# Unread matrix products ahead of four stages of a two-layer attention and experts kernel, and one projection moved forward

## The chip, the cores and the metric

The kernel runs on one core of one Trainium2 chip, as one program. The metric is the device time of one execution in microseconds (us). Three executions of the kernel before took 1533.29, 1536.22 and 1537.31 us; the median is 1536.22 us. The engines are named as in the profile: PE (TensorE), PEld (its weight loads), DVE (VectorE), ACT (ScalarE), POOL (GpSimd), SP (SyncE, which here only issues DMAs).

## The reference

4096 tokens (32 blocks of 128) of width 256 go through two layers, each an attention and a mixture of experts, every one added to its input:

```python
x = x + L0_xattn(layernorm(x), ctx, ctx, ...)   # 16 heads, masked by token id
x = x + L0_ffn(layernorm(x), ...)               # router, top 2 of 8 experts, width 1024
x = x + L1_xattn(layernorm(x), ctx, ...)        # two attentions and a gate
x = x + L1_ffn(layernorm(x), ...)               # top 2 of 8, at most 640 tokens for each expert
```

## The kernel before, in words

The program has four stages, one after the other on every engine. Each engine runs a list of instructions written out in full; the order within an engine is the order of the calls in the code, and between engines only semaphores order the work.

- Stage A (`first_attention`, from 0 to about 400 us) runs the first attention over 32 blocks, writes the normalised rows to DRAM, and scatters token numbers to the slots of the experts. `a_pe` starts with two small transposes (line 684), and then takes the blocks in a software pipeline.
- Stage B (`first_experts`, about 400 to 826 us) runs 71 blocks of expert rows. POOL gathers slot numbers (`load_ids`, line 1175, counted in `i_ld`) and then rows (`gather`, line 1183). ACT and DVE split the rows into a high and a low f16 part. SP turns them by a DMA transpose (`xT`). PE makes the hidden layer in `up(j)` (12 products of 512 columns, line 1342, two halves, each counted in `up_done`). ACT applies silu to each half (line 1300, `silu_done`), casts the high part (line 1305, `hi_done`); DVE makes the low part (line 1273, `lo_done`); SP transposes the hidden rows (`hT`); PE makes `down(j)` (24 products, line 1355). The loop in `b_pe` calls `up(j + 1)`, `down(j - 1)` and `fold(pe, j)` for j from -1 on. The addresses of the weights hang on the expert's number, which PE loads into a register and adds up in register instructions between the products.
- Stage C (`second_attention`, about 826 to 1158 us) runs the second attention over 32 blocks. `from_ctx(b)` projects context rows into PSUM bank 0 (line 1822, counted in `ts_done`) and bank 2 (line 1828, `vs_done`). ACT takes the first out (`ctx_out`, `ts_out`), DVE the second (`vs_out`). `transpose_x(b)` (line 1849) and `from_rows(b)` do the same for the normalised rows of the stage, which wait for the gathers of the expert rows of stage B (`yg_ld`, line 1639) and for the normalisation on DVE, POOL and ACT (lines 1981 to 1989, 1648 to 1652, 1713). `scores(b)` (lines 1869 and 1872) needs both. ACT's exponential is line 1744, and `transpose_p` is line 1880. In the kernel before, `from_ctx(1)` stands behind `scores(0)`.
- Stage D (`second_experts`, about 1158 to 1530 us) runs 8 experts with 640 slots each. POOL first clears `rowsum` (line 2217, `d_clear`), waits for the slot numbers and gathers 5 blocks of 128 rows for expert 0 (line 2225). PE transposes each block (`transpose_x`, line 2269), ACT and DVE split it into f16 parts (lines 2331 and 2374), and both must be done before the next transpose may write the same bank. The hidden width is taken in 8 units; `up(e, p, fc, q)` (line 2285) makes a unit's products in three pieces q of 256, 256 and 128 columns, 12 products each; `down` is line 2298. ACT's silu is line 2339.

## Time and profile before

| | us |
|---|---|
| median of three runs (1533.29 to 1537.31) | 1536.22 |
| the profiled execution | 1534.38 |
| its span, first to last instruction | 1532.6 |
| outside its span | 1.8 |
| PE busy (89%) | 1356.7 |
| PEld busy (72%) | 1100.2 |
| DVE busy (55%) | 847.2 |
| ACT busy (53%) | 816.1 |
| POOL busy (44%) | 671.5 |

Start times below are us from the start of the span. Busy time of PE is modelled: products overlap, and one product's duration is longer than the distance to the next one. "[7.44 <-ACT qeo L558]" in a row means that the engine had been idle for 7.44 us, and that ACT's instruction on `qeo` at line 558 released it.

### The profile page before, as it was taken

What the parts mean: (1) busy time and instruction counts of PE and PEld (TensorE: products, weight loads), DVE (VectorE), ACT (ScalarE), POOL (GpSimd) and SP (SyncE); (2) the same over time, 40 slices, a digit from 0 to 9 for tenths busy, and PEclk for the clock granted to TensorE, in tenths of its full rate; (3) what the DMA queues carried; (4) which work ended last, traced back from release to release, by engine and by line L of the source; (5) the groups of instructions that cost most, each with busy time, mean ns of one, the idle gap of its engine ahead of it and who ended that gap; (6) DMA issues with size and microseconds to landing.
All of it is one profiled execution on the core that took longest, in us unless ns stands there. A gap on an engine that the chain in (4) does not pass through costs nothing.

```text
span 1532.6 us, 37450 instructions
## 1 busy us (share of the span) xinstructions
PE 1356.7 (89%) x12922; PEld 1100.2 (72%) x12922; DVE 847.2 (55%) x2350; ACT 816.1 (53%) x1904; POOL 671.5 (44%) x935
## 2 busy tenths in 40 slices
PE   5999999997169999999996899999982999999996
PEld 4787777775136666667664888888871888888985
DVE  4787788776423222332231677777762566666663
ACT  3787778775035555554552555555541545454442
POOL 3234545454453333333302456666655344444322
PEclk8999999999579999999998999999995999999998
DMA  3333435442059999988885223332222333343331
GB/s 113 111 113 98 121 94 103 108 90 54 21 112 178 201 193 182 183 169 149 161 160 121 69 84 84 83 84 83 81 64 57 109 124 113 123 130 104 127 104 50
DMA packets 280856, 172.76 MB, mean 113 GB/s; under 512 B 212990, under 2 KB 259424, under 8 KB 280676
## 3 DMA queue, kind: packets, MB, share of 16 engines
q1 hardware_dynamic: 257940, 134.65, 38.8%
q0 software_dynamic: 18608, 32.14, 7.7%
q10 hardware_dynamic: 4128, 3.57, 0.8%
q8 instruction: 112, 1.84, 0.6%
q14 instruction: 68, 0.56, 0.2%
HBM read 93.40 MB, written 31.80 MB: 82 GB/s over the span
## 4 chain that ended last, share of the span: by engine, by line
PE 81%; issue 4%; ACT 4%; DVE 3%; DMA 3%; POOL 2%; another core or an unknown queue 1%; ACTq 0%; SPq 0%; DVEq 0%; POOLq 0%
PE psum L2285 14%; PE psum L1355 12%; PE psum L1342 11%; PE psum L2298 7%; PE psum L1822 4%; PE psum L1903 4%; PE psum L1828 3%; PE psum L747 2%; PE psum L805 2%; PE psum L734 2%; PE psum L708 2%; PE psum L822 2%; PE psum L1893 2%; PE psum L808 2%; PE psum L786 2%
## 5 line engine op out<-in xcount | busy, mean ns | idle before, releaser
L1273 DVE SCALAR_TENSOR_TENSOR b_h<-b_hid,b_h 128x1024 f16<-128x1024 f32 x71 | 87.0, 1225 | 280.6 <-ACT b_h L1305 274.7
L2285 PE MATMUL psum<-d_xT,d_w 128*128 128x256 f16 (+1 forms) x2304 | 231.5, 257 | 5.3 <-DVE d_xT L2374 2.9
L1342 PE MATMUL psum<-arena,b_xT 128*128 x852 | 200.2, 386 | 28.0 <-DMA b_xT<-b_x 27.6
L2285 PEld LDWEIGHTS psum<-d_xT,d_w 128*128 128x128 f16 x2304 | 200.1, 99 | 24.1 <-DVE d_xT L2374 2.5
L1355 PE MATMUL psum<-arena,b_hT 128*128 x1704 | 200.5, 274 | 13.9 <-DMA b_hT<-b_h 8.8
L1355 PEld LDWEIGHTS psum<-arena,b_hT 128*128 128x128 f16 x1704 | 166.0, 98 | 52.9 <-issue 20.2
L1342 PEld LDWEIGHTS psum<-arena,b_xT 128*128 128x128 f16 x852 | 84.3, 99 | 119.1 <-issue 36.6
L1300 ACT ACTIVATE b_hid<-psum 128x512 f32<-128x512 f32 x142 | 84.7, 597 | 136.3 <-PE psum L1342 85.6
L1183 POOL DMA_INDIRECT b_xg<-dram_normed,b_gi x71 | 67.1, 945 | 205.2 <-DVE b_x L1266 193.6
L2339 ACT ACTIVATE d_sg<-psum 128x256 f32<-128x256 f32 (+1 forms) x192 | 65.8, 348 | 147.7 <-PE psum L2285 136.3
L2384 DVE SCALAR_TENSOR_TENSOR d_hf<-psum,d_sg 128x256 f32<-128x256 f32 (+1 forms) x192 | 71.0, 379 | 107.8 <-ACT d_sg L2339 89.3
L2298 PE MATMUL psum<-d_w,d_h 128*128 128x256 f16 x960 | 115.3, 273 | 2.3 <-issue 1.6
L602 ACT ACTIVATE pT<-psum,amc 128x512 f32<-128x512 f32 x128 | 77.6, 689 | 48.5 <-PE psum L734 43.3
L2298 PEld LDWEIGHTS psum<-d_w,d_h 128*128 128x128 f16 x960 | 91.2, 98 | 15.3 <-issue 4.8
L1639 POOL DMA_INDIRECT c_yg<-dram_expert_rows,c_gi x64 | 65.0, 1015 | 69.9 <-DMA dram_expert_rows<-b_ys 54.9
L949 DVE TENSOR_REDUCE mx<-psum 128x4 f32<-128x512 f32 x128 | 79.4, 682 | 27.4 <-PE psum L708 25.5
L2242 POOL DMA_INDIRECT d_rowsum<-out,d_gi x40 | 44.7, 1118 | 91.6 <-PE psum L2285 67.8
L1175 POOL DMA_INDIRECT b_gi<-dram_ids,ypos x71 | 68.6, 967 | 31.4 <-issue 31.4
L2247 POOL DMA_INDIRECT out<-d_rowsum,d_gi x40 | 41.8, 1045 | 92.4 <-DVE d_rowsum L2399 85.1
L1305 ACT ACTIVATE b_h<-b_hid 128x1024 f16<-128x1024 f32 x71 | 75.0, 1057 | 4.7 <-DMA b_hT<-b_h 2.5
L1674 POOL DMA_INDIRECT dram_ids<-c_gsidw,c_gsidx x64 | 68.0, 1063 | 19.4 <-issue 19.4
L477 POOL DMA_INDIRECT dram_ids<-tokens,gsidx x64 | 67.5, 1054 | 12.6 <-issue 12.6
(316 smaller groups left out, 2930.4 us busy)
## 6 DMA issues: line engine op xcount, KB each, us to landing
d_wst<-in_L_w SPq DMA_DIRECT2D x64, 384.0 KB
stage<-in_L_w SPq DMA_DIRECT2D x32, 512.0 KB
dram_expert_rows<-b_ys SPq DMA_DIRECT2D x71, 128.0 KB
ctxT<-in_ctxT SPq DMA_DIRECT2D x64, 128.0 KB
dram_normed<-xn SPq DMA_DIRECT2D x64, 128.0 KB
x<-in_x SPq DMA_DIRECT2D x32, 128.0 KB, 5.8
dram_x<-xnew SPq DMA_DIRECT2D x32, 128.0 KB
c_x<-dram_x SPq DMA_DIRECT2D x32, 128.0 KB
```

Of the source, the lines that this page charges most:

```text
L602: act.activation(pT[:, r, :, :].rearrange("p j q -> p (j q)"), psum[:, SB + r, :], ACT.Exp, bias=amc[:, b:b + 1]).then_inc(exp_done[r], 1)
L949: i = dve.tensor_reduce(mx[:, r, :], psum[:, SB + r, :].rearrange("p (j k) -> p j k", j=HB), AX.X, ALU.max)
L1175: pool.indirect_dma_start(gi[:, j % NX, :], None, ids[0], bass.IndirectOffsetOnAxis(ap=ypos[:, j:j + 1], axis=0)).then_inc(i_ld[j % NX], 16)
L1273: dve.scalar_tensor_tensor(out=h16[:, p, 1, :], in0=hid[:, p, :], scalar=H_SCALE, in1=h16[:, p, 0, :], op0=ALU.mult, op1=ALU.subtract).the ...
L1300: act.activation(hid[:, p, half * 512:(half + 1) * 512], psum[:, 1 + 2 * p + half, :], ACT.Silu, scale=1.0 / (X_SCALE * W_SCALE)).then_inc ...
L1305: act.activation(h16[:, p, 0, :], hid[:, p, :], ACT.Copy, scale=H_SCALE).then_inc(hi_done, 1)
L1342: i = pe.matmul(psum[:, 1 + 2 * p + half, :], xT[:, j % NT, px, c, :], weights(e, c, pw, half * 512, 512), start=(n == 0), stop=(n == len( ...
L1355: i = pe.matmul(psum[:, 6 + p, 0:D], hT[:, p, ph_, c, :], weights(e, 2 + c // 4, pw, (c % 4) * D, D), start=(n == 0), stop=(n == len(terms ...
L1674: pool.indirect_dma_start(ids[1], bass.IndirectOffsetOnAxis(ap=gsidx[:, g % 3, at:at + 1], axis=0), gsidw[:, g % 3, at, :], None, bounds_c ...
L2285: i = pe.matmul(psum[:, q, m * n:(m + 1) * n], w16[:, fc % RING, pw, col:col + P], xT[:, p, px, c, at:at + n], start=(k == 0), stop=(k == ...
L2298: i = pe.matmul(psum[:, NQ + k, 0:D], h16[:, fc % 2, ph_, k * P:(k + 1) * P], w16[:, fc % RING, pw, 2 * DC * P:UW], start=(fc == 0 and t = ...
L2384: dve.scalar_tensor_tensor(out=hf[:, fc % 2, at:at + n], in0=psum[:, q, n:2 * n], scalar=H_SCALE / (X_SCALE * W_SCALE), in1=sg[:, fc % 2, ...
```

## The change

`keep_on(pe, bank, n)` issues n products of the f16 identity with itself, 128 columns each, into a bank of PSUM that is overwritten before anybody reads it. Each has its own weight load. It is called in stage A behind the two small transposes (36), in stage B ahead of `up(0)` once the first slot numbers are there (60) and between `up(1)` and `up(2)` in three parts (24, 20, 40) that each wait for a step of block 0, in stage C ahead of the first transpose, once the first gathered rows are there (36), and in stage D behind POOL's clearing of `rowsum` (56) and behind each of the five transposes of expert 0 (10 each). That is 332 products. In stage C `from_ctx(1)` comes directly behind `from_ctx(0)`, with ACT's `ctx_out(1)` and DVE's `vs_out(0)` and `vs_out(1)` moved to the front of their lists as well.

```diff
--- before.py
+++ after.py
@@ -172,6 +172,11 @@
         def due(v):
 
             return not isinstance(v, int) or v > 0
+
+        def keep_on(pe, bank, n):
+
+            for _ in range(n):
+                pe.matmul(psum[:, bank, 0:P], ident16[:, :], ident16[:, :], start=True, stop=True)
 
         class Steps:
 
@@ -683,6 +688,7 @@
                 for k in range(2):
                     i = pe.transpose(psum[:, 2, k * NB:(k + 1) * NB], rows_f[:, k, :], ident[0:NB, 0:NB])
                 i.then_inc(rowt_done, 1)
+                keep_on(pe, 7, 36)
 
                 def penalty(b, r, n):
 
@@ -1356,8 +1362,15 @@
                                           start=(n == 0), stop=(n == len(terms) - 1))
                         i.then_inc(down_done, 1)
 
+                pe.wait_ge(i_ld[0], 16)
+                keep_on(pe, 5, 60)
                 for j in range(-1, N_B + 1):
                     up(j + 1)
+                    if j == 0:
+
+                        for steps, n in ((silu_done, 24), (hi_done, 20), (lo_done, 40)):
+                            pe.wait_ge(steps, 2 if steps is silu_done else 1)
+                            keep_on(pe, 5, n)
                     down(j - 1)
                     fold(pe, j)
 
@@ -1792,16 +1805,18 @@
                         act.wait_ge(w_ready, g)
                     act.activation(ge[:, 0:n], gd[:, 0:n], ACT.Exp).then_inc(ge_ready, 1)
 
+                ctx_out(0)
+                ctx_out(1)
                 normalise_x(0)
                 xnT_out(0)
-                ctx_out(0)
                 normalise_x(1)
                 rows_out(0)
                 xnT_out(1)
                 for b in range(NB + 2):
                     expo(b)
                     normalise_x3(b - 2)
-                    ctx_out(b + 1)
+                    if b > 0:
+                        ctx_out(b + 1)
                     gate(b - 1)
                     x2T_out(b - 2)
                     pT_out(b)
@@ -1831,7 +1846,9 @@
                 def from_ctx(b):
                     if inside(b):
                         pe.wait_ge(ctx_ld[b % 2], nth(b))
-                        if due(b):
+                        if b == 1:
+                            pe.wait_ge(ts_out, 1)
+                        if due(b - 1):
                             pe.wait_ge(tc_out, b)
                         project(ms, ctxT[:, b % 2, :, :], 0).then_inc(ts_done, 1)
                         if due(b):
@@ -1852,7 +1869,7 @@
                 def from_rows(b):
                     if inside(b):
                         pe.wait_ge(xnT_ready, b + 1)
-                        pe.wait_ge(ts_out, b + 1)
+                        pe.wait_ge(ts_out, max(b + 1, 2))
                         project(mc, xT[:, b % 2, :, :], D).then_inc(tc_done, 1)
                         if due(b):
                             pe.wait_ge(vc_ready, b)
@@ -1950,6 +1967,9 @@
                 pe.wait_ge(fold_out, 2)
                 pe.wait_ge(col_out, 1)
                 from_ctx(0)
+                from_ctx(1)
+                pe.wait_ge(yg_ld[0], 32)
+                keep_on(pe, 5, 36)
                 transpose_x(0)
                 from_rows(0)
                 transpose_x(1)
@@ -1957,7 +1977,8 @@
                     if last_of(b - 3) is not None:
                         count(last_of(b - 3))
                     scores(b)
-                    from_ctx(b + 1)
+                    if b > 0:
+                        from_ctx(b + 1)
                     gate(b - 1)
                     transpose_x3(b - 2)
                     transpose_p(b)
@@ -2122,8 +2143,9 @@
                         dve.wait_ge(scat[g % 3], scattered(g - 3))
                     dve.tensor_copy(gsidx[:, g % 3, 0:2 * n], gslot[:, 0:2 * n]).then_inc(slot_ready, 1)
 
+                vs_out(0)
+                vs_out(1)
                 add_experts(0)
-                vs_out(0)
                 add_experts(1)
                 vc_out(0)
                 for b in range(NB + 3):
@@ -2138,7 +2160,8 @@
                     top(b - 2)
                     if last_of(b - 2) is not None:
                         hots(last_of(b - 2))
-                    vs_out(b + 1)
+                    if b > 0:
+                        vs_out(b + 1)
                     vc_out(b + 1)
                     residual(b - 1)
             return c_sync, c_pool, c_act, c_pe, c_dve, load_weights, scaled, first_rows, fold_pe, fold_act, fold_dve
@@ -2306,6 +2329,7 @@
                             if e == 0 and fc == 0:
                                 for k in range(2 * q, min(2 * q + 2, CBLK)):
                                     transpose_x(0, 0, k)
+                                    keep_on(pe, NQ + CBLK - 1, 10)
                             if q == NQ - 1 and 1 <= fc <= CBLK and is_expert(e + 1):
                                 pe.wait_ge(h_ready, NQ * (e * FC + fc))
                                 transpose_x(e + 1, 1 - p, fc - 1)
@@ -2314,6 +2338,8 @@
                             up(e, p, fc, q)
                         down(e * FC + fc - 1, (fc - 1) % FC, e)
 
+                pe.wait_ge(d_clear, 1)
+                keep_on(pe, NQ + CBLK - 1, 56)
                 for e in range(E):
                     body(e, e % 2)
                 down(E * FC - 1, FC - 1, E - 1)
```

## Rows read from the trace of the kernel before

**Rows 1.** The page's slices of the span: the granted clock of PE, in tenths.
```profile
PEclk8999999999579999999998999999995999999998
```

**Rows 2.** Windows: stretch, its length, busy us of each engine, clock, DMA share, GB/s.
```profile
422.30:427.20 4.90, 4.79 (x12) 1.86 (x13) 0.42 (x1) 2.30 (x3) 3.68 (x5) 0.50 0.45 104
427.20:437.50 10.30, 6.91 (x39) 3.40 (x37) 1.56 (x2) 2.56 (x4) 8.17 (x8) 1.00 0.53 115
...
833.40:843.60 10.20, 4.59 (x16) 3.74 (x17) 3.57 (x10) 2.72 (x7) 5.32 (x9) 0.50 0.18 53
...
1178.90:1185.00 6.10, 3.98 (x17) 2.57 (x18) 0.85 (x2) 0.77 (x2) 2.12 (x3) 0.50 0.24 65
1185.00:1188.40 3.40, 1.44 (x12) 0.93 (x11) 0.85 (x2) 0.77 (x2) 1.93 (x2) 1.00 0.13 39
...
1340.00:1360.00 20.00, 20.00 (x209) 18.24 (x207) 12.01 (x24) 9.96 (x22) 4.95 (x5) 1.00 0.36 114
```

**Rows 3.** Timeline of stage A: start, us, engine line op out<-in, count, idle before.
```profile
17.94 0.75 POOL L463 TENSOR_SCALAR other<-tokr,tokc 128x128 f32<-128x128 f32 x1 [9.48 <-DMA tokr<-dram_tokens]
...
22.98 0.66 PE L776 MATMUL psum<-ident,xn 128*128 128x128 f32 x2 [7.44 <-ACT qeo L558]
```

**Rows 4.** Timeline of the start of stage C.
```profile
833.89 0.48 DVE L1981 SCALAR_TENSOR_TENSOR c_ytmp<-c_yg,routew,c_x 128x256 f32<-128x256 f32 x1 [14.48 <-DMA c_yg<-dram_expert_rows,c_gi]
...
837.93 0.69 PE L1849 MATMUL psum<-ident,xn 128*128 128x128 f32 x2 [9.53 <-ACT xn L1713]
...
839.70 2.04 PE L1822 MATMUL psum<-c_xT,c_Wq_c 128*128 128x128 f32 x8 [1.08 <-ACT c_tsT L1728]
...
841.03 0.60 ACT L1713 ACTIVATE xn<-c_x,rstd 128x256 f32<-128x256 f32 x1 [1.47 <-POOL rstd L1652]
...
841.54 1.92 PE L1828 MATMUL psum<-c_Wv_c,c_xT 128*128 128x257 f32 x4
...
844.57 1.06 PE L1822 MATMUL psum<-ctxT,c_Wq_s 128*128 128x128 f32 x8
...
847.20 0.45 PE L1880 MATMUL psum<-ident,c_pr 128*128 128x128 f32 x2 [0.70 <-DVE c_pr L2010]
```

**Rows 5.** Timeline of the start of stage D.
```profile
1171.52 1.17 POOL L2217 MEMSET d_rowsum<- 128x1280 f32 x1 [1.78 <-DMA dram_ids<-c_gsidw,c_gsidx]
...
1178.97 0.69 PE L2269 MATMUL psum<-ident,d_xg 128*128 128x128 f32 x2 [20.65 <-DMA d_xg<-dram_normed,d_gi]
...
1182.37 2.72 PE L2285 MATMUL psum<-d_xT,d_w 128*128 128x256 f16 x12 [1.02 <-DVE d_xT L2374]
...
1192.93 3.89 PE L2285 MATMUL psum<-d_xT,d_w 128*128 128x256 f16 x24 [0.33 <-DVE d_hf L2384]
...
1196.88 0.83 PE L2285 MATMUL psum<-d_xT,d_w 128*128 128x128 f16 x12
...
1199.18 2.78 PE L2285 MATMUL psum<-d_xT,d_w 128*128 128x256 f16 x24
```

**Rows 6.** Timeline of the start of stage B.
```profile
411.80 1.00 POOL L1175 DMA_INDIRECT b_gi<-dram_ids,ypos  x1 [10.06 <-issue]
...
422.40 10.31 PE L1342 MATMUL psum<-arena,b_xT 128*128 x36 [27.58 <-DMA b_xT<-b_x]
...
423.71 1.28 ACT L1300 ACT_TABLE_LOAD   x1
...
434.99 0.60 ACT L1300 ACTIVATE b_hid<-psum 128x512 f32<-128x512 f32 x1 [5.42 <-remote]
...
436.11 2.30 PE L1355 MATMUL psum<-arena,b_hT 128*128 x15 [3.39 <-DMA b_hT<-b_h]
...
440.38 0.94 POOL L1175 DMA_INDIRECT b_gi<-dram_ids,ypos  x1 [0.30 <-issue]
...
444.10 0.60 ACT L1300 ACTIVATE b_hid<-psum 128x512 f32<-128x512 f32 x1 [8.52 <-remote]
```

**Rows 7.** Line 1342 alone, 415 to 460 us: durations in ns, min/median/max.
```profile
L1342 PEldq FUSED_REGOPS  x41: 3/46/692, 422.3 to 460.0; - x41
```

## The prediction

> **What bounds the kernel now.** I read the slices of the clock first, then windows over the stretches where it is low, then the timeline there. The slices show PE at 8 to 10 tenths except where one stage ends and the next begins, near 400, 830 and 1170 us [rows 1]. Inside the last stage PE is the bound: 20.00 us busy in a window of 20 [rows 2]. So a microsecond that PE gains at the start of stage D is not given back later. At the starts PE waits for gathered rows, for 27.58 us in stage B, 9.53 us in C and 20.65 us in D [rows 4 to 6], and begins its first work at a clock of 0.50, which is 1.2 GHz: 422.3 to 427.2, 833.4 to 843.6 and 1178.9 to 1185 us [rows 2]. The change can win only the time by which this first work is slower than at 2.4 GHz, and only where that work, not another engine, ends last.
>
> **Price of an unread product.** At the full clock, 12 products of 128 columns took 0.83 us and 24 of 256 took 2.78 us [rows 5]. The tail is the same, so 35 steps of 128 columns cost 1.95 us: 0.056 us each. At half clock I take twice that, 0.11 us; the 12 of 256 columns in 2.72 us [rows 5] agree (22 steps of 0.11 us and a tail of 0.3).
>
> **Stage A, 36 products.** 4.0 us behind the two small transposes, with up to 0.7 us of delay for the first block's transpose. What stands behind is block -2's work of the pipeline, and then PE idles for 7.44 us until 22.98 us, since POOL's mask waited 9.48 us for a DMA until 17.94 [rows 3]. Both the gain and the delay end in that idle time. Value 0. Bounds: without this cover a delay of 0.7 us; a gain is excluded, as the DMA chain hangs on DVE.
>
> **Stage B, 60 products and then 84.** The first slot numbers land between 412.8 and 415.6 us (POOL's first issue ends at 412.8 [rows 6]). Sixty products at half clock are 6.6 us, so they end at 422.2 at the latest, just ahead of `up(0)` at 422.40 [rows 6]. The 24 products of `up(0)` and `up(1)` then run at up to twice the speed. But ACT loads its table until 424.99 [rows 6] and takes out the first half only after that, so the second half's silu moves from 427.6 to 425.8 at best: 1.8 us. That is lost or kept at the next wait. What is late next is not the clock: ACT stood for 5.42 us until 434.99 and for 8.52 us until 444.10 for an event that the profile can't name [rows 6], though the 36 products that it waited for are recorded as over at 432.71. In the same stretch PE's register instructions between the products took up to 692 ns against a median of 46 [rows 7]. POOL was issuing indirect DMAs all that time, 23 from 411.80 to 440.38, one each 1.25 us [rows 6]; the hold-up begins after the clock rose at 427.2 and ends some 3 us after POOL's last issue. If it ends by POOL's schedule, an earlier start gains nothing: value 0. The 84 products between `up(1)` and `up(2)` wait for block 0's low part, ready about 430.5. At full clock the last 40 are 2.2 us and `up(2)` some 2.6, so PE is at `down(0)` at 435.4, and its data came at 436.11 [rows 6]: hidden by 0.7 us. At half clock they are 4.4 and 5.1 us: 3.9 us late, in front of ACT's second wait that lasted to 444.10. Bounds of stage B: 12 us gained (if the hold-up goes) to 8 us lost (below).
>
> **Stage C, 36 products and the moved projection.** At 0.50, the two transposes took 0.69 us, the projection 2.04 and the value product 1.92 [rows 4]. At full clock the pair of transposes takes 0.45 and the eight projection products 1.06 [rows 4]; the value product goes to about 1.0. But the chain goes by the later of PE and the normalisation of block 1. ACT's `xn` of block 1 starts at 841.03, released by POOL [rows 4], and neither POOL's list nor its gathers move, so it ends at 841.63 as before. The second transpose started at 843.25, behind the value product (841.54 + 1.92, less overlap) [rows 4]; now it can start at 841.65. Scores of block 0 and all that follows move by 1.6 us. The 36 products (4.0 us from about 833.9) end at 837.9, when the transpose comes (837.93 [rows 4]); if they end late, the delay is under 0.3 us. The moved `from_ctx(1)` goes to PE's idle time before the rows. From where it stood (844.57, 1.06 us and some 1.0 more [rows 4]) it takes nothing off the path, as PE still waited 0.70 us for `c_pr` [rows 4] that DVE makes. It passes no DMA. On ACT, `ctx_out(0)` and `ctx_out(1)` come in idle time; on DVE the two `vs_out` wait for products that end by 831, before the rows at 833.89 [rows 4]. Value 1.6 us gained; bounds 0.5 lost (late products) to 2.5 gained (all of 0.24 + 0.98 + 0.9 and a little more, if `xn` were earlier too).
>
> **Stage D, 56 and 50 products.** POOL's clearing ends at 1172.69, and 56 products at half clock take 6.2 us, to 1178.9; the first transpose is at 1178.97 [rows 5]. The ten behind each transpose lie under the trip through ACT and DVE that the next transpose waits for anyway (1.0 us at full clock with the transpose itself, against 1.7 us between the first two). Gain along the path, piece by piece at 2.4 GHz: two transposes ahead of the first `up`, 0.25 each; `up` of piece 0 from 2.72 to half of 2.78 and a tail, about 1.5: 1.2; piece 1, which ran at mixed clock, 0.6; last transpose, 0.2; then 24 products of the next unit from 3.89 to 2.78 [rows 5], of which the transpose among them leaves 1.2. Sum 3.7 us. Pieces on ACT (table load, silu) keep their length. Bounds: 0 (clock stays low) to 4.5.
>
> A page of the Trainium skill speaks against both starts. The row first: between 1185 and 1188.4 us the clock was 1.00, PE worked 1.44 us in pieces with waits between them, and it was 0.50 again afterwards [rows 2]; so a burst with waits lost the full clock once it had it. "TensorE: Matmul & The Clock Gate", section "HAM oscillation — how this bites in real kernels", says the same of kernels whose products come in short bursts between waits. By that rule the starts stay bursts, the sum is the 2.5 us of rival 3 and the time 1533.7; by the ten products that fill the waits of stage D it is 5.3 us. The granted clock of the one stretch bears the rule out, but there the waits were empty.
>
> **Sum.** 0 + 0 + 1.6 + 3.7 = 5.3 us. Against the profiled execution's own time of 1534.38 that gives 1529.1; it is 1.8 us under the median of the runs, 1536.2, so for the median 1530.9. I say 1531.
>
> **Rivals.**
> 1. *The hold-up in stage B gets longer: slower.* Its place is PE's instruction stream while POOL issues its 23 DMAs. It began 1.3 us after the clock rose. With a warm PE from about 420 us and 60 dense products in front, it would begin some 8 us earlier (420 against 428.5), before the silu of block 0, and still end with POOL at about 444. Then block 0's hidden rows are transposed only when block 1's were before, and the pipeline is one block behind at least. A block is 24 products of 256 columns and 12 of 512, 48 steps of 256 columns at 0.109 us: 5.2 us. A second block lost would be 10.4; I take 8: 1531 + 8 = 1539. It decides from 5.3 us, where it eats the gains of C and D. For it: 692 ns instructions only with the dense warm stream [rows 7]. Against it: the unread products have no register instructions between them.
> 2. *The hold-up goes away.* Spacing PE's work differently could avoid it. Then `lo_done` of block 1 comes at 433 instead of 447, less 2 us for the DMA queue: 11 to 12 us, and 1531 - 11 = 1520. For it: nothing but that its cause is unknown.
> 3. *The clock doesn't stay up.* In stage D it falls after the first transposes, as at 1188.4; in stage C PE is now idle from about 843 to 845.6, where `from_ctx(1)` had been, so the clock may fall there instead, and the next projection pair costs 2 us more, half of it under waits. Stage D then keeps 1.9 of 3.7 and stage C 0.6 of 1.6: 2.5 us, 1533.7.
> 4. *The unread products do not raise the clock at all*: stage B to D as before, small delays: 1536. Speaks against it: plain f16 products raised the clock at 427.2 [rows 2].
>
> **How the numbers follow.** This kernel's measurement can tell 0.3%, 4.6 us: faster is under 1531.6. Chances: forecast 0.42, rival 1 0.20, rival 2 0.13, rival 3 0.20, rival 4 0.05. The forecast's own spread is about 3 us either way, since stage B's wait is not exact; some 0.30 of its 0.42 lies under 1531.6. With rival 2 and a little of rival 3 that is 0.45 faster. Same, 1531.6 to 1540.8: the rest of the forecast, rivals 3 and 4, and the lighter part of rival 1 (a loss of up to 8 us in stage B ends inside), 0.41. Slower 0.14, where two blocks or more are lost. The range: 1522 leaves out the lower part of rival 2, 1539.5 the upper part of rival 1; the likeliest case alone has 1528 to 1534.
>
> **What would show it.** Right: the granted clock at 1.0 from about 837 and 1178 us on; 843.25 for the second transpose of stage C becoming 841.6; the piece of 12 products in stage D at 1.5 us and its successor of 24 at 2.8. ACT's two unnamed waits in stage B end near 435 and 444. Wrong: those waits shorter or later by over 3 us, a clock of 0.5 within 1179 to 1190 or 844 to 851, or a first transpose in stage D later than 1179.5.

## The result, and the profile after

| | before | after |
|---|---|---|
| median of 20 runs each | 1532.99 us (1526.23 to 1538.14) | 1540.82 us (1536.64 to 1546.74) |
| profiled execution | 1534.38 us | 1544.04 us |
| its span | 1532.6 us | 1542.3 us |

The ratio of after to before is 1.0056, with a 95% interval of 1.0043 to 1.007: the change made the kernel slower, by 7.8 us between the medians and by 8.6 us by the ratio. The forecast was 1531, with a range of 1522 to 1539.5. From one group of runs to the next the kernel before took from 1509 to 1544 us, so kernels are compared within their group only, by the ratio; where an experiment's difference is given in us, it is the ratio times the group's median of the kernel before.

The page of the kernel after, busy time of PE and the slices of its clock:

```profile
PE 1382.9 (90%) x13244; PEld 1128.4 (73%) x13244; DVE 848.7 (55%) x2350; ACT 816.7 (53%) x1904; POOL 670.6 (43%) x935
...
PEclk8999999998579999999999899999996999999998
```

PE is busy 26 us longer than before, and the clock's slices hardly differ from [rows 1]. It executes 322 products more, 13244 against 12922: the change adds 36 + 60 + 84 + 36 + 56 + 50 = 322, not 332. Where the time went is read from the start times of the same step in both traces. The profiled execution after was 9.7 us longer: 5.4 us of it were there at POOL's first slot gather of stage B (411.80 and 417.20), 6.3 came up to the `down` of block 10, 5.9 in the rest of stage B. Stage C gave back 1.8 and stage D 6.1.

Of the 6.1 us of stage D only 2.1 lie where the change could reach, from the first transpose to the 97th product of `up`. The other 4.1 come behind it and are not the change's: in all 17 traces this rest of stage D takes either 312.6 to 313.9 us or 317.1 to 317.9, and in each group of the experiments all kernels lie on one level, with and without the change; only this first pair of traces lies on both. The 5.9 us in the rest of stage B can't be put down to the change either: it takes 334.3 us before and 340.3 after, and from 334.1 to 341.7 in the other kernels that leave POOL alone there (331.8 to 333.5 with POOL held, below).

The start of stage B after, a timeline (columns as in [rows 3]; line 1348 is `up`, 1361 `down`, 179 the unread products):

```profile
417.20 1.00 POOL L1181 DMA_INDIRECT b_gi<-dram_ids,ypos  x1 [8.80 <-issue]
...
420.06 5.07 PE L179 MATMUL psum<-ident 128*128 128x128 f16 x60 [18.59 <-DMA b_gi<-dram_ids,ypos]
...
428.02 3.84 PE L1348 MATMUL psum<-arena,b_xT 128*128 x17 [2.89 <-issue]
...
434.33 0.38 PE L1348 MATMUL psum<-arena,b_xT 128*128 x1 [1.72 <-issue]
...
442.31 0.94 POOL L1181 DMA_INDIRECT b_gi<-dram_ids,ypos  x1 [0.31 <-issue]
...
445.53 0.59 PE L1348 MATMUL psum<-arena,b_xT 128*128 x1 [1.51 <-issue]
447.05 1.08 ACT L1306 ACTIVATE b_hid<-psum 128x512 f32<-128x512 f32 x2 [16.55 <-PE psum L1348]
...
448.19 7.65 PE L179 MATMUL psum<-ident 128*128 128x128 f16 x84 [2.08 <-ACT b_hid L1306]
...
458.27 2.78 PE L1361 MATMUL psum<-arena,b_hT 128*128 x24
```

Beside [rows 6]: the 60 products end in time, and `up(0)` begins at full clock. After 17 products of `up` PE gets one product each 2.1 us, while POOL issues a DMA each 1.25 us; "issue" says that PE waited for nothing that the profile shows. It ends some 5 us after POOL's last issue. ACT's silu of block 0 waits 16.55 us, where ACT had waited twice, 5.42 and 8.52 us. Then the 84 products take 7.65 us, and `down(0)` is at 458.27 instead of 436.11.

Windows of the kernel after (columns as in [rows 2]), the ones of stage B first:

```profile
428.00:432.00 4.00, 3.84 (x17) 1.68 (x18) 0.42 (x1) 1.70 (x2) 3.07 (x4) 1.00 0.47 113
432.00:446.00 14.00, 3.35 (x7) 0.61 (x6) 0.00 (x0) 0.00 (x0) 8.52 (x9) 0.68 0.18 47
```
```profile
845.00:848.00 3.00, 2.93 (x17) 2.04 (x15) 0.44 (x2) 1.25 (x4) 0.95 (x1) 1.00 0.33 96
848.00:851.40 3.40, 0.00 (x0) 0.00 (x0) 0.41 (x1) 0.00 (x0) 2.48 (x4) 0.80 0.39 119
851.40:855.50 4.10, 4.01 (x37) 3.82 (x38) 3.16 (x8) 0.60 (x1) 2.35 (x5) 0.50 0.19 57
...
1191.40:1200.00 8.60, 4.51 (x63) 3.95 (x62) 0.85 (x2) 0.77 (x2) 4.79 (x6) 1.00 0.49 165
```

From 432 to 446 PE starts 7 products and 6 weight loads, and ACT and DVE nothing at all. In stage C the moved projection ends at full clock before 848; PE is empty until the rows land, and the 36 products and the first transpose run at 0.50. The starts of stages C and D, timelines after, for [rows 4] and [rows 5]:

```profile
851.47 0.48 DVE L2002 SCALAR_TENSOR_TENSOR c_ytmp<-c_yg,routew,c_x 128x256 f32<-128x256 f32 x1 [3.06 <-DMA c_yg<-dram_expert_rows,c_gi]
...
851.49 4.02 PE L179 MATMUL psum<-ident 128*128 128x128 f16 x36 [3.55 <-DMA c_yg<-dram_expert_rows,c_gi]
...
855.44 0.69 PE L1866 MATMUL psum<-ident,xn 128*128 128x128 f32 x2
...
856.60 2.08 PE L1837 MATMUL psum<-c_xT,c_Wq_c 128*128 128x128 f32 x8 [0.47 <-ACT c_xT L1733]
...
860.18 0.43 PE L1866 MATMUL psum<-ident,xn 128*128 128x128 f32 x2
```
```profile
1188.63 4.58 PE L179 MATMUL psum<-ident 128*128 128x128 f16 x56 [14.43 <-POOL d_rowsum L2240]
...
1194.75 0.44 PE L2292 MATMUL psum<-ident,d_xg 128*128 128x128 f32 x2 [1.54 <-DMA d_xg<-dram_normed,d_gi]
...
1199.27 1.47 PE L2308 MATMUL psum<-d_xT,d_w 128*128 128x256 f16 x12 [1.94 <-DVE d_xT L2400]
...
1207.75 2.78 PE L2308 MATMUL psum<-d_xT,d_w 128*128 128x256 f16 x24 [0.94 <-DVE d_hf L2410]
```

### The profile page after: what moved, and what is told of

It is laid out like the page before. It is cut to its first block, busy times and chain, and to the rows that moved or that the text cites. A ratio compares the mean times of both kernels' runs of the same rounds, so it can differ in the third digit from the quotient of the medians.

```text
span 1542.3 us, 38095 instructions
## 1 busy us (share of the span) xinstructions
PE 1382.9 (90%) x13244; PEld 1128.4 (73%) x13244; DVE 848.7 (55%) x2350; ACT 816.7 (53%) x1904; POOL 670.6 (43%) x935
## 4 chain that ended last, share of the span: by engine, by line
PE 80%; DVE 5%; issue 5%; DMA 4%; ACT 4%; POOL 2%; another core or an unknown queue 0%; ACTq 0%; SPq 0%; DVEq 0%; POOLq 0%
PE psum L2308 14%; PE psum L1348 11%; PE psum L1361 11%; PE psum L2321 7%; PE psum L1837 3%; PE psum L1843 3%; PE psum L1920 3%; PE psum L811 2%; PE psum L753 2%; PE psum L740 2%; PE psum L828 2%; DMA b_hT<-b_h 2%; PE psum L714 2%; PE psum L814 2%; PE psum L1910 2%
## 5 line engine op out<-in xcount | busy, mean ns | idle before, releaser
L2308 PE MATMUL psum<-d_xT,d_w 128*128 128x256 f16 (+1 forms) x2304 | 227.1, 255 | 3.6 <-DVE d_xT L2400 2.7
L2308 PEld LDWEIGHTS psum<-d_xT,d_w 128*128 128x128 f16 x2304 | 198.3, 98 | 22.6 <-issue 3.2
L1361 PEld LDWEIGHTS psum<-arena,b_hT 128*128 128x128 f16 x1704 | 166.4, 98 | 43.9 <-issue 10.8
L1348 PEld LDWEIGHTS psum<-arena,b_xT 128*128 128x128 f16 x852 | 83.6, 98 | 105.1 <-issue 22.6
L2321 PEld LDWEIGHTS psum<-d_w,d_h 128*128 128x128 f16 x960 | 91.0, 98 | 11.7 <-issue 1.0
L955 DVE TENSOR_REDUCE mx<-psum 128x4 f32<-128x512 f32 x128 | 79.5, 683 | 22.8 <-PE psum L714 22.7
```

The costliest lines, as they stand in the source:

```text
L955: i = dve.tensor_reduce(mx[:, r, :], psum[:, SB + r, :].rearrange("p (j k) -> p j k", j=HB), AX.X, ALU.max)
L1348: i = pe.matmul(psum[:, 1 + 2 * p + half, :], xT[:, j % NT, px, c, :], weights(e, c, pw, half * 512, 512), start=(n == 0), stop=(n == len( ...
L1361: i = pe.matmul(psum[:, 6 + p, 0:D], hT[:, p, ph_, c, :], weights(e, 2 + c // 4, pw, (c % 4) * D, D), start=(n == 0), stop=(n == len(terms ...
L2308: i = pe.matmul(psum[:, q, m * n:(m + 1) * n], w16[:, fc % RING, pw, col:col + P], xT[:, p, px, c, at:at + n], start=(k == 0), stop=(k == ...
L2321: i = pe.matmul(psum[:, NQ + k, 0:D], h16[:, fc % 2, ph_, k * P:(k + 1) * P], w16[:, fc % RING, pw, 2 * DC * P:UW], start=(fc == 0 and t = ...
```

## The experiments

While it issues them back to back, PE and ACT get their instructions slowly, about one each 0.70 us on PE (a weight load, a register instruction and a product make the 2.1 us above). PE lives on what it has in hand; every unread product takes two instructions of that. **Rivals.** The clock: a warm, dense PE brings the hold-up on. The products' own time: the 84 stand in the way.

The table has all kernels; a group is named by the median of the kernel before in it. "Start of B" is from POOL's first slot gather to the `down` of block 10; "start of C" from `add_experts(0)` to the first softmax (its maximum on DVE); "D" from its first transpose to its last product, "its start" from there to the 97th product of `up`. The ratios come from 6 to 20 executions of each kernel, these columns from the one that was profiled, and that one lies up to 8.6 us from its kernel's median.

| kernel | group | ratio to before (95%) | A, block 31 at | start of B | start of C | D | its start |
|---|---|---|---|---|---|---|---|
| before | 1533 | | 386.6 | 87.8 | 10.9 | 340.8 | 23.0 |
| after | 1533 | 1.0056 (1.0043 to 1.007) | 393.2 | 94.0 | 10.1 | 334.6 | 21.0 |
| without B's products | 1536 | 1.0007 (0.9987 to 1.0028) | 389.6 | 87.6 | 10.2 | 333.7 | 20.8 |
| 60 of B alone | 1536 | 1.0043 (1.002 to 1.0065) | 397.2 | 94.3 | 10.6 | 336.0 | 23.2 |
| 15 wide in B | 1536 | 1.0006 (0.9988 to 1.0025) | 390.7 | 89.2 | 11.7 | 338.4 | 24.6 |
| POOL held | 1536 | 0.9914 (0.989 to 0.9937) | 392.1 | 77.3 | 11.8 | 337.0 | 23.0 |
| 36 of A alone | 1541 | 1.0036 (1.0021 to 1.0051) | 396.1 | 88.6 | 11.7 | 340.9 | 23.2 |
| 84 of B alone | 1541 | 1.0031 (1.0017 to 1.0045) | 389.9 | 93.9 | 11.8 | 340.4 | 23.0 |
| C and D alone | 1541 | 0.9988 (0.9969 to 1.0007) | 391.3 | 88.5 | 9.0 | 338.7 | 21.1 |
| after, POOL held | 1541 | 0.9947 (0.9926 to 0.9969) | 392.0 | 79.8 | 9.1 | 339.9 | 22.6 |
| held, C warm, D | 1509 | 0.9934 (0.9915 to 0.9953) | 378.7 | 76.9 | 9.0 | 333.0 | 20.4 |
| 9 wide in A | 1509 | 1.0002 (0.9983 to 1.0021) | 382.8 | 79.3 | 10.8 | 335.6 | 23.0 |
| POOL spaced | 1509 | 1.0005 (0.9986 to 1.0024) | 380.9 | 77.4 | 10.3 | 333.9 | 21.3 |
| spaced, again | 1544 | 1.0005 (0.9989 to 1.0021) | 394.4 | 90.1 | 11.8 | 342.2 | 24.3 |
| held, C warm, D, again | 1544 | 0.9887 (0.9865 to 0.9908) | 394.2 | 77.2 | 9.7 | 339.3 | 22.3 |
| 9 wide in A, again | 1544 | 0.9995 (0.9981 to 1.0008) | 386.4 | 88.9 | 10.5 | 340.8 | 23.2 |
| held, again | 1544 | 0.9902 (0.9884 to 0.992) | 391.2 | 78.7 | 10.6 | 342.5 | 24.7 |

**Without B's products.** The two groups of calls taken out of `b_pe`; the rest as after.

```diff
-                pe.wait_ge(i_ld[0], 16)
-                keep_on(pe, 5, 60)
...
-                    if j == 0:
...
-                            keep_on(pe, 5, n)
```

> The changed kernel without both groups of unread products of stage B (60 and 84); those of stages A, C and D and the moved projection stay. Theory 1, the loss is made in stage B (from its first slot-number gather to its tenth down it lost 6.3 us, and some 3 more by its end): the time is that of the kernel before less what C (0.8 us) and D (2.5 us at its start) gained, so 2 to 4 us faster than before. Rival, the 36 products of stage A shift its pipeline (stage A was 6.6 us longer in the profile after): then this kernel is still 2 to 4 us slower than before, and its block 31 of stage A ends near 393 us and not near 387.

The 0.56% are gone: the loss hangs on stage B's products. But the gain of 2 to 4 us wasn't there either (1.1 us slower, interval 2.0 faster to 4.3 slower), and neither was the rival's loss of 2 to 4. So something else in the rest may cost.

**60 of B alone**, and **15 wide**: the kernel before with only

```diff
+                pe.wait_ge(i_ld[0], 16)
+                keep_on(pe, 5, 60)
```
or, in the same place, 15 products with a moving side of 512 columns (the identity read four times by a stride of 0):
```diff
+            wide = rows(ident16[:, :], 4)
...
+                pe.matmul(psum[:, bank, :], ident16[:, :], wide, start=True, stop=True)
```

> The kernel before with only the 60 unread products of stage B. Theory 1, instruction supply: while POOL issues its indirect DMAs back to back PE gets one instruction each 0.70 us as soon as the ones it has in hand are used up; before this happened after some 140 instructions (from 438 us), in the kernel after at 432 us after some 176, of which 120 belonged to the 60 products. So these 60 alone are enough: PE's instructions 0.70 us apart from about 427 us (time of the kernel before) to about 443, inside up(1), the first lo part of block 1 a block (5.2 us) later than in the kernel before, and 4 to 7 us slower. Rival, the loss came of the 84 products (7.65 us at half clock between up(1) and up(2)): then this kernel takes the time of the one before within 1 us, or is 1 us faster.

> As the kernel with the 60 products alone, but the same columns in 15 products of 512 (30 instructions instead of 120), at the same place and for the same time on PE. Theory 1, the number of instructions counts: PE runs short no earlier than without unread products, so no block is lost, the time is that of the kernel before within 1.5 us, and the clock is full from about 421 us all the same. Rival, the warm clock (PE's own rate and its register instructions at full clock) brings the hold-up on: then it is as slow as the kernel with 60, 4 to 7 us over the kernel before.

Timeline of the 60, then of the 15 wide with its window:

```profile
440.27 0.38 PE L1347 MATMUL psum<-arena,b_xT 128*128 x1 [1.72 <-issue]
...
451.60 0.60 ACT L1305 ACTIVATE b_hid<-psum 128x512 f32<-128x512 f32 x1 [16.60 <-PE psum L1347]
```
```profile
418.24 5.21 PE L185 MATMUL psum<-ident 128*128 128x512 f16 x15 [19.20 <-DMA b_gi<-dram_ids,ypos]
...
446.28 0.37 PE L1366 MATMUL psum<-arena,b_hT 128*128 x1 [1.73 <-issue]
```
```profile
426.00:434.20 8.20, 8.04 (x36) 3.44 (x36) 1.99 (x3) 4.26 (x6) 6.37 (x7) 1.00 0.39 91
```

The 60 kept PE busy for 5.38 us, the 15 for 5.21, in the same place. The 60 cost 0.43%, the 15 nothing that can be measured. With the 15 all 36 products of `up(0)` to `up(2)` went through in 8.04 us at clock 1.00, and the shortage began only in `down(0)`, as in the kernel before; with the 60 it began 17 products into `up`, though the clock there was the lower one:

```profile
432.50:438.00 5.50, 5.24 (x17) 2.10 (x18) 0.43 (x1) 1.70 (x2) 4.05 (x5) 0.74 0.44 108
```

So the clock is not the cause: with the same columns, the same time on PE and the full clock earlier, what differs is the number of instructions. ACT's hold-up came with the 15 too (8.66 us until 440.01), as in the kernel before; what the 60 added is PE's shortage inside `up`. The total is the weaker half of this: the two were compared in one group only, and their intervals overlap a little (from 1.002 on, and up to 1.0025).

**POOL held.** The kernel before, and POOL's issues tied to PE's pace:

```diff
                 for j in range(N_B):
+                    if 5 <= j < N_B:
+                        pool.wait_ge(up_done, 2 * (j - 4))
                     load_ids(j + 2)
                     gather(j)
```

> The kernel before with POOL held back in stage B: from block 5 on its next two indirect DMAs wait until up(j-4) is done; no unread products. POOL then issues some 12 back to back and not 23, and the rest at PE's pace of 5.2 us a block. Theory 1, PE is short of instructions because of POOL's back-to-back issues: the stretch with PE's instructions 0.70 us apart (438 to 444 us) goes, ACT's two unnamed waits (5.42 and 8.52 us) shrink, and the kernel is 5 to 12 us faster than before. Rival, the hold-up has another cause (the DMAs of weights, the address arithmetic of PE): the stretch stays where it was, the time within 1.5 us, or slower if the gathers now come late for PE.

The first burst has 12 issues instead of 23; the kernel is 0.86% faster, 13 us, and 0.98%, 15 us, in another group, each a little more than forecast. ACT's two waits ahead of block 1's silu, line 1302 here, are now 0.26 and 0.90 us:

```profile
435.80 0.60 ACT L1302 ACTIVATE b_hid<-psum 128x512 f32<-128x512 f32 x1 [0.26 <-PE psum L1344]
437.29 0.60 ACT L1302 ACTIVATE b_hid<-psum 128x512 f32<-128x512 f32 x1 [0.90 <-PE psum L1344]
```

So the largest loss at this place is in the kernel before too, and holding POOL back ends it.

**36 of A alone, 84 of B alone, C and D alone**: the kernel before with one part of the change each; for C and D all of the change's diff but these lines:

```diff
                 i.then_inc(rowt_done, 1)
+                keep_on(pe, 7, 36)
...
                     up(j + 1)
+                    if j == 0:
+
+                        for steps, n in ((silu_done, 24), (hi_done, 20), (lo_done, 40)):
+                            pe.wait_ge(steps, 2 if steps is silu_done else 1)
+                            keep_on(pe, 5, n)
```

> The kernel before with only the 36 unread products of stage A. Theory, they do nothing: block 0 of stage A ends at 49.3 us as in both profiles, the spread of stage A's end (386.6 to 397.2 us over six kernels, two with these products at 393.2 and 389.6, four without at 386.6, 397.2, 390.7 and 392.1) is chance, and the time is that of the kernel before within 1.5 us. Rival, they cost what the kernel without stage B's products lacks against its expected 2 to 4 us gain: then 2 to 5 us slower.

> The kernel before with only the 84 unread products of stage B (168 instructions of PE between up(1) and up(2)). Theory 1, every instruction counts while PE gets one each 0.70 us: the products stand in PE's way from about 433 us, less than half are through by the time that POOL's burst ends (about 441), and down(0) comes 8 to 12 us later than its 436.1; block 1's lo part keeps its time or comes earlier, so 3 to 6 us slower in all. Rival, they lie in idle time (they wait for ACT and DVE, and down(0) for the transposed rows): the time of the kernel before within 1.5 us.

> The kernel before with the changes of stages C and D alone: the moved projection and 36 products in C, 56 and 50 products in D. From the profiles so far C's start takes 0.8 to 0.9 us less (add_experts to the first softmax 10.88 us before, 10.07 after) and stage D 334.6 and 333.7 us from its first transpose to its last product with the change, 336.0 to 340.8 without it. Theory: C gains 0.8 and D 2.5 to 4: 3 to 5 us faster. Rival: D's shorter time is chance, as it gains only 1 us at its first piece, and what is left is within 1.5 us of the kernel before.

The 36 products of stage A cost 5.5 us, a little more than the rival's 2 to 5, where I had forecast nothing. The 84 cost 4.8 us, as theory 1 said, and put `down(0)` 40.0 us behind POOL's first gather instead of 24.3: later by 15.7 us, not by the 8 to 12 forecast. C and D alone are 1.8 us faster (4.8 faster to 1.1 slower): less than the theory's 3 to 5, and not to be told from the rival's nothing. In the 36's trace, stage A shows the mark of stage B's hold-up:

```profile
345.86 1.08 POOL L482 DMA_INDIRECT dram_ids<-tokens,gsidx  x1 [0.18 <-issue]
...
347.87 1.00 POOL L482 DMA_INDIRECT dram_ids<-tokens,gsidx  x1 [0.17 <-issue]
349.17 0.97 POOL L482 DMA_INDIRECT dram_ids<-tokens,gsidx  x1 [0.30 <-issue]
351.33 0.60 ACT L616 ACTIVATE oT<-psum 128x512 f32<-128x512 f32 x1 [6.77 <-remote]
...
351.98 1.11 PE L762 MATMUL psum<-ident,oT 128*128 128x128 f32 x4 [6.22 <-ACT oT L616]
```

ACT stands 6.77 us for something that the profile can't name, while POOL issues three scatters close together. In other traces such a wait of 3 to 7 us falls on other blocks between 345 and 395 us, and block 31 ends anywhere from 386 to 397 (397.2 in the kernel with the 60 of B alone, which has no product in stage A). So the 36's loss is shown by the totals, and not where in stage A it falls.

**9 wide in A**: the same columns as the 36, in 9 products of 512.

```diff
                 i.then_inc(rowt_done, 1)
+                keep_on_wide(pe, 7, 9)
```

> The kernel before with stage A's unread columns in 9 products of 512 instead of 36 of 128: the same time on PE, 18 instructions instead of 72. The 36 products alone made the kernel 0.36% slower (5.5 us, 0.21 to 0.51%), though block 0 of stage A kept its time (49.32 us) and the loss came in blocks 24 to 31. Theory 1, the number of instructions of PE ahead of the pipeline shifts where its later shortages fall: with 18 the time is that of the kernel before within 2 us. Rival, the products' time or the clock shifts the pipeline: then 3 to 7 us slower, as with the 36.

> Stage A's unread columns in 9 products of 512, the rest as the kernel before. The 36 products of 128 cost 0.36% where the kernel before took 1541 us; the 9 cost 0.02% where it took 1509. If the number of instructions counts: within 2 us of the kernel before, also where it takes 1533 to 1541 us. If their time on PE does: 3 to 7 us slower.

Twice nothing (1.0002 and 0.9995), where the 36 cost 0.36%. The first of the two came in the group without the hold-up and says little; the second came with it, though not beside the 36. The same columns in 18 instructions instead of 72 cost nothing that can be measured. Which later step pays for the 72 isn't shown; one profile each can't separate it from the spread of stage A.

**After, POOL held.** The whole change with the two lines of the held POOL.

> The changed kernel with all its unread products, and POOL held back in stage B from block 5 on as in the kernel that took 12 us less. Theory 1, the unread products of stage B cost time only because PE is short of instructions while POOL issues back to back: then they cost nothing here (the 60 end before the rows, the 84 lie in PE's wait for the transposed hidden rows, but for 1 to 2 us), and the time is that of the held kernel less C's and D's gains, 11 to 16 us faster than before. Rival, they cost time of their own (7.65 us at half clock between up(1) and up(2)): then it is 3 to 8 us slower than the held kernel, 4 to 9 us faster than before.

8.2 us faster than before: the rival's forecast (4 to 9), not theory 1's (11 to 16). B's start takes 79.8 us, against 77.3 and 78.7 held without products and 94.0 in the kernel after: of the 6.3 us that the products cost there, 1.2 to 2.6 are left when POOL is held. The rest of the 5 to 7 us by which this kernel lags behind the held one is not traced; the 36 of stage A are in it. The hold-up is short here, but it is there: PE runs short after 18 products of `up`, at the same place as in the kernel after, and has its instructions again 3.3 us after the last issue of POOL's first burst, at 431.19:

```profile
433.05 0.38 PE L1350 MATMUL psum<-arena,b_xT 128*128 x1 [0.88 <-issue]
434.45 1.24 PE L1350 MATMUL psum<-arena,b_xT 128*128 x5 [1.02 <-issue]
```

**POOL spaced.** Behind each issue of blocks 2 to 11 POOL fills an unused tile twice:

```diff
                     load_ids(j + 2)
+                    if 2 <= j < 12:
+                        space(2 * j - 4)
                     gather(j)
+                    if 2 <= j < 12:
+                        space(2 * j - 3)
```

> The kernel before with POOL's indirect DMAs of stage B spaced: behind each from block 2 to block 11 POOL fills an unused tile twice (some 1 us), and waits for nothing. The issues come some 2.4 us apart instead of 1.25, in the same number and order. Theory 1a, what holds PE and ACT up is the rate of POOL's issues: ACT's waits of 5.42 and 8.52 us go, and the kernel is 5 to 12 us faster than before. Theory 1b, it is their number ahead of use, whatever the rate: the stretch comes later but is as long, and the time is within 2 us of the kernel before or slower.

> POOL's indirect DMAs of blocks 2 to 11 of stage B spaced by two fills of an unused tile each, as before. The first comparison came where the kernel before took 1508.8 us, and a kernel of that group with POOL unchanged in stage B (the one with 9 wide products) had no wait of ACT over 3 us at the start of stage B: it could not tell. Where the kernel before shows its usual 1533 to 1541 us: theory 1a (the rate of the issues) 5 to 12 us faster than before; theory 1b (their number ahead of use) within 2 us or slower.

The first comparison couldn't tell, as there was no hold-up in its group (the 9 wide of that group: 79.3 us at the start of B, no wait of ACT over 3 us after the first rows). In the second the time was again that of the kernel before: theory 1b's forecast, and not the 5 to 12 us of 1a. The windows of this trace show where the time went:

```profile
444.60:473.90 29.30, 29.21 (x206) 20.16 (x207) 11.65 (x18) 16.66 (x29) 25.75 (x39) 1.00 1.01 181
473.90:482.90 9.00, 8.86 (x58) 5.48 (x56) 2.08 (x4) 2.78 (x5) 6.80 (x8) 1.00 0.93 156
483.00:492.00 9.00, 2.19 (x7) 0.67 (x7) 0.00 (x0) 0.00 (x0) 5.58 (x6) 0.74 0.18 45
```

As long as the issues came 2.2 us apart, PE was never short (29.21 us busy of 29.3), and block 4's low part was ready 37.6 us after the first gather instead of 48.4. The spacing ended at 473.97; POOL then issued each 1.25 us to 489.16, and 9 us into that PE had 7 products in 9 us, and ACT none:

```profile
492.67 0.38 ACT L1323 ACTIVATE b_ys<-psum 128x256 f32<-128x256 f32 x1 [14.34 <-remote]
```

The 11 us gained at the start were lost there. So the hold-up moves to where POOL issues back to back, and both the time and the later place are what 1b forecast. That it is the rate and not the number of blocks by which POOL leads is likely, but not shown. For it: in the kernel after PE ran short with five blocks gathered and one `up` done, a lead of four, while the held kernels have a lead of up to five through all of stage B and three of them no hold-up. Against it: while the issues were spaced the lead stayed at four or less, so this run doesn't part the two.

**Held, C warm, D.** POOL held, nothing in A and B, stage D as after, and in stage C PE kept busy across the wait for the rows:

```diff
                 from_ctx(1)
-                pe.wait_ge(yg_ld[0], 32)
-                keep_on(pe, 5, 36)
+                keep_on(pe, 5, 60)
+                pe.wait_ge(yg_ld[0], 32)
+                keep_on(pe, 5, 56)
```

> POOL held back in stage B as before; no unread products in stages A and B; stage D as in the changed kernel; in stage C the moved projection, 60 unread products right behind it (before the rows land) and 56 after. In the changed kernel the clock fell again at 850.0 us, between the moved projection (over at 847.9) and the 36 products (from 851.49), and the first transposes ran at half clock. Theory: with PE kept busy across the wait for the rows the clock is full from the rows to the first softmax, and that stretch (from add_experts, 10.88 us before, 10.07 in the kernel after, 8.95 in the one with C and D alone) takes 8.5 to 9.2 us; with D's 3 us and the held POOL's 12 the kernel is 14 to 18 us faster than before. Rival: what fills the stretch is the chain through DVE, POOL and ACT and not the clock, and it stays at 10; 12 to 15 us faster.

> POOL held back in stage B, stage C with the moved projection and 60 and 56 products, stage D as in the changed kernel. At 1508.8 us for the kernel before it was 10 us faster. If the hold-up is back (kernel before at 1533 to 1541 us): 14 to 18 us faster than before, and 3 to 6 us faster than the held kernel without C and D, which runs beside it. Rival, C and D bring nothing that can be measured: as fast as the held kernel within 1.5 us.

> The kernel before with POOL held back from block 5 of stage B on, as in the run that was 12 us faster, beside the spaced one: if the hold-up is there it is 9 to 14 us faster again, and tells whether this comparison is one in which the spaced kernel can be judged; if it is not there, it is within 3 us of the kernel before.

The timeline of the second of these at the start of stage C:

```profile
823.99 1.03 PE L1837 MATMUL psum<-c_Wv_s,ctxT 128*128 128x257 f32 x4
824.86 3.98 PE L179 MATMUL psum<-ident 128*128 128x128 f16 x65
...
829.88 2.95 PE L179 MATMUL psum<-ident 128*128 128x128 f16 x50 [0.51 <-issue]
832.68 0.39 PE L1860 MATMUL psum<-ident,xn 128*128 128x128 f32 x2
834.76 1.16 PE L1831 MATMUL psum<-c_xT,c_Wq_c 128*128 128x128 f32 x8 [1.70 <-ACT c_xT L1727]
```

The transposes take 0.39 us and the projection 1.16, against 0.69 and 2.08 in the kernel after. Yet the start of C takes 9.0 and 9.7 us, no less than with C and D alone (9.0), where the clock was 0.50 from 842.6 to 849.4. The first lies in the theory's range and the second nearer to the rival's 10; that the chain through ACT, DVE and POOL fills the rest is the likely reason and isn't shown. It is the fastest version: 0.66% under the kernel before in the group without the hold-up, and 1.13%, 17 us, in the one with it; there it is 2.3 us under the held kernel, a difference inside the intervals and under the 3 to 6 forecast.

## Why the prediction was wrong, point by point

**Stage A, 0 us.** Failed. Block 0 was not delayed (49.31 and 49.33 us), as forecast, and still the 36 products cost 5.5 us. The step looked for a cover at the place where they stand; what they spend, 72 instructions, has its price later.

**Stage B, 0 us.** This is the step that failed most: "if it ends by POOL's schedule, an earlier start gains nothing: value 0". It does end by POOL's schedule (3 to 6 us after the last issue of a burst), and an earlier start isn't free: 120 instructions of unread products make PE run short while it is still in `up`, where ACT waits for it. 0.43% (6.6 us) measured for the 60 alone, 0.31% (4.8 us) for the 84 alone. Each lies inside the step's bound of 8 us lost; the value 0 was wrong. I read the register instructions of 692 ns [rows 7] as the mark of a dense warm stream; in the kernel after these took 46 ns, and it was the weight loads and products that came late. The rows that told more were ACT's two waits for nothing named [rows 6]: two engines late at once, which nothing of PE's own work explains.

**Rival 1** is what happened, with its sign, its place and about its size: it gave 8 us for stage B alone and 1539; the start of B lost 6.3 us and the total came to 1540.8 against 1533.0. Its reason, the clock, was wrong: the wide products had the same clock and lost nothing. So was its start 8 us earlier: ACT began to stand 17.8 us after POOL's first issue before, and PE ran short 15.0 us after it in the kernel after. Against it I had set that "the unread products have no register instructions between them"; that had no bearing. Its 0.20 was too small, as the cover of the 84 products was 0.7 us by my own sum.

**Rival 2**, the hold-up goes away: not by this change, but its price of 11 to 12 us was about right, as holding POOL shows (13 and 15 us).

**Stage C, 1.6 us.** The size was about right: over the profiles of all groups but the one at 1509 us, the start of C takes 9.6 us on average with the changes (five kernels) and 11.3 without (nine), 1.7 less. In the profile after it was 0.8, since the clock was lost between 848 and 851.4, while PE stood 3.55 us for the rows, a place that the prediction hadn't named. The second transpose came 8.7 us behind the first rows instead of 9.4 in the kernel before and 7.8 as forecast. The place that rival 3 did name, the idle time where `from_ctx(1)` had been, lost the clock as well, and the eight projection products behind it took 1.91 us instead of 1.06:

```profile
863.97 0.69 PE L1897 MATMUL psum<-ident,c_pr 128*128 128x128 f32 x2 [2.47 <-DVE c_pr L2031]
864.45 1.91 PE L1837 MATMUL psum<-c_xT,c_Wq_c 128*128 128x128 f32 x8
```

So rival 3 held in stage C of this execution. The Trainium skill, page "TensorE: Matmul & The Clock Gate", section "HAM oscillation — how this bites in real kernels", warns of just such bursts with waits between. The window of stage C agrees (0.80 while PE stood 3.55 us, then 0.50).

**Stage D, 3.7 us.** The right way, but mis-sized: to the 97th product of `up` the five kernels with the changes take 21.6 us on average (20.8 to 22.7) and the nine without 23.6 (23.0 to 24.7), again without the group at 1509: 2.0 gained. The whole of D, 337.2 against 339.9, says 2.6, but the two levels of its rest are in that. The piece of 12 took 1.47 us as forecast and the later 24 took 2.78; the first transpose was found at full clock. Two terms failed. The ten products were to lie under the trip through ACT and DVE; but with them the first `up` starts 3.9 to 4.7 us behind the first transpose, and 3.4 in every kernel without them. In the kernel after, ACT took out the second pair of transposes at 1198.28, 1.5 us after it was over; what held ACT is not shown:

```profile
1196.36 0.41 PE L2292 MATMUL psum<-ident,d_xg 128*128 128x128 f32 x2 [0.61 <-issue]
...
1198.28 0.38 ACT L2357 ACTIVATE d_xT<-psum 128x256 f16<-128x256 f32 x1 [2.52 <-PE psum L2292]
```

And the clock: it stayed at 1.00 in four of the six kernels with these products, this one among them, and fell for a while in "after, POOL held" and in "held, C warm, D, again", though ten products stood in each wait and none that was left lasted over 2.29 us. The windows of the second:

```profile
1168.90:1175.80 6.90, 3.90 (x57) 3.36 (x55) 0.81 (x2) 0.77 (x2) 4.04 (x5) 0.99 0.63 210
1175.80:1179.20 3.40, 3.21 (x17) 2.51 (x18) 0.04 (x1) 0.03 (x1) 0.00 (x0) 0.50 0.00 0
```

There the piece of 12 took 2.72 us again, so rival 3 held in stage D of those two. C and D together measured 1.8 us alone, and 2.3 us on top of the held POOL with the 60 and 56 products in C.

**Sum.** In place of 0 + 0 + 1.6 + 3.7 gained, the parts measured alone are 5.5 lost (A), 6.6 and 4.8 lost (the 60 and the 84, which overlap in one hold-up), and 1.8 gained. They don't add: together they cost 7.8 us.

## What to carry to other kernels

Filling an engine's wait isn't free because the engine is idle: count the filler's instructions, and use few wide ones; 9 and 15 products of 512 columns cost nothing that could be measured where 36 and 60 of 128 cost 0.4%. When two engines stand at once for something that the profile can't name, look at what a third issues back to back in that stretch; here holding it back gave more than twice the 5.3 us that the clock was forecast to give. And a total that doesn't move can hide a gain and a loss: what the spaced kernel won and lost is seen only in windows. Before a stage's time in two traces is put down to a change, compare a part of it that the change doesn't touch: the rest of stage D moved by 4 us by itself, more than the change won there.

## What the runs showed of the hardware

In the nine traces with the hold-up and with POOL neither held nor spaced, it began 15 to 19 us after POOL's first issue of stage B, the issues 1.25 us apart: PE got instructions about 0.70 us apart, or a multiple of that, and ACT none for up to 13 us in which it didn't wait for PE, until 3 to 6 us after the last issue of the burst. Behind the spaced issues it began 9 us into the burst and held ACT for 14.34 us. With a first burst of 12 to 14 issues it did not come in three held kernels, and lasted some 2 us on PE in the fourth, the one with the unread products; with 2.2 us between issues it did not come. The path isn't shown. It isn't a wait for a load of instructions: in the kernel after the hold-up ended by 448, and from 425 to 455 us its DMA queues have no packet of that kind, of which the whole execution has 182 in two queues:

```profile
## 3 DMA queue, kind: packets, MB, share of 16 engines
q1 hardware_dynamic: 3713, 0.92, 15.9%
q0 software_dynamic: 684, 1.18, 14.3%
```

In the group in which the kernel before took 1508.8 us the hold-up was missing in the kernel with 9 wide products, with 27 issues in one burst; what differs there is open; the record gives that group and the one at 1541 the same chip number. Open too is what sets the two levels of the rest of stage D, and why 72 instructions in stage A's first 20 us cost time in the end. Every execution here comes with a span and a clock, so all were recorded, and no run tells whether the hold-up is there without that.
